# Local attention loop of a hybrid network on one core: scores of head pairs on two 64-row tiles, in a reordered step

## What is computed

```python
def local_attention(q, k, v):            # 8 heads of 64, windows of 64 tokens
    # each query sees its own window and the one before it
    sim = jnp.einsum('bhwid,bhwjd->bhwij', bq, bk)
    mask = (i < j) | (i > j + WINDOW) | (j == -1)
    sim = jnp.where(mask, -jnp.finfo(sim.dtype).max, sim)
    attn = jax.nn.softmax(sim, axis=-1)
    return jnp.einsum('bhwij,bhwjd->bhwid', attn, bv)

def _layer(x, wqkv, qs, ksc, wo, lg, lb, w1, b1, w2, b2):
    h = shift_token(x)
    q, k, v = jnp.split(h @ wqkv, 3, axis=-1)      # then to heads
    q, k = rotary_xpos(l2norm(q) * qs, l2norm(k) * ksc)
    x = x + local_attention(q, k, v) @ wo
    h = layernorm(shift_token(x)) * lg + lb
    a, g = jnp.split(h @ w1 + b1, 2, axis=-1)      # 341 wide each
    return x + (a * gelu(g)) @ w2 + b2
```

## Time and profile before

| | us |
|---|---|
| median of 3 timed runs | 2193.34 |
| lowest and highest of them | 2189.93, 2195.23 |
| the profiled execution, its device time | 2203.51 |
| the profiled execution, its span from first to last instruction | 2201.7 |

### The profile page before, as it was taken

One profiled execution on the slowest core, in us unless ns is written; L12 is line 12 of the kernel. 1 busy time (PEld: TensorE's weight loads), 2 busy tenths in 40 slices (PEclk: granted clock), 3 DMA queues, 4 the chain that ended last, 5 costly groups with the idle time before them and its releaser, 6 DMA issues.

```text
span 2201.7 us, 34222 instructions
## 1 busy us (share of the span) xinstructions
PE 1819.8 (83%) x10946; PEld 1445.6 (66%) x11003; DVE 1407.5 (64%) x3623; ACT 942.4 (43%) x2559; POOL 454.2 (21%) x350
## 2 busy tenths in 40 slices
PE   7999966654566888898888799999968988888887
PEld 6888854222355777676676677777847766776676
DVE  4655689556896666676757445655547767566673
ACT  3444422110213555546454363353225464555544
POOL 2200010000013333332424100000014324233340
PEclk9999977555778999999999899999879999999998
DMA  3000000000100000000000000000000000000000
GB/s 133 0 0 0 1 0 0 1 0 0 48 0 1 3 1 2 3 2 4 1 2 1 3 1 0 0 0 0 0 1 4 2 2 1 4 2 3 2 1 22
DMA packets 15104, 13.89 MB, mean 6 GB/s; under 512 B 11286, under 2 KB 14138, under 8 KB 14650
## 3 DMA queue, kind: packets, MB, share of 16 engines
q1 hardware_dynamic: 15034, 13.01, 1.8%
HBM read 9.87 MB, written 1.05 MB: 5 GB/s over the span
## 4 chain that ended last, share of the span: by engine, by line
PE 45%; issue 30%; DVE 16%; ACT 7%; POOL 1%; DVEq 1%; POOLq 0%; ACTq 0%
PE bank L1558 5%; PE bank L1526 4%; PE bank L1546 4%; PE bank L1695 3%; PE bank L1642 3%; PE bank L1537 3%; DVE arena_attn L916 3%; PE bank L1655 2%; PE bank L1677 2%; DVE arena_ffn L901 2%; PE bank L1720 2%; PE bank L1699 2%; DVE probT L686 2%; ACT L1264 2%; PE bank L1743 2%
## 5 line engine op out<-in xcount | busy, mean ns | idle before, releaser
L534 POOL TENSOR_TENSOR arena_ffn<-arena_ffn 128x1024 f32<-128x1024 f32 x60 | 141.5, 2359 | 561.7 <-DVE arena_ffn L901 561.7
L686 DVE COPY probT<-bank 128x512 f32<-128x512 f32 x288 | 197.1, 684 | 70.7 <-PE bank L1537 70.4
L518 POOL TENSOR_TENSOR rstd<-var,mhalf 128x2 f32<-128x2 f32 x48 | 33.4, 696 | 902.6 <-DVE var L641 902.6
L1546 PE MATMUL bank<-vF,probT 128*128 128x64 f32 x1536 | 203.0, 276 | 1.7
L1546 PEld LDWEIGHTS bank<-vF,probT 128*128 128x128 f32 x1536 | 191.3, 196 | 12.9 <-DVE probT L686 12.2
L530 POOL TENSOR_TENSOR inv<-ssq,mhalf 128x16 f32<-128x16 f32 x64 | 188.2, 2940 | 33.6 <-DVE ssq L910 29.9
L1526 PE MATMUL bank<-arena_setup 128*128 128x192 f32 (+1 forms) x1024 | 171.6, 300 | 7.2 <-ACT arena_setup L1317 5.6
L679 DVE TENSOR_REDUCE nmaxF<-bank 128x2 f32<-128x384 f32 (+1 forms) x192 | 114.7, 597 | 88.9 <-PE bank L1526 88.9
L1368 ACT ACTIVATE arena_conv<-bank,nmaxF 128x192 f32<-128x192 f32 x256 | 105.6, 420 | 147.9 <-DVE nmaxF L679 95.1
L1526 PEld LDWEIGHTS bank<-arena_setup 128*128 128x128 f32 x1024 | 154.3, 191 | 11.8 <-issue 0.4
L897 DVE TENSOR_TENSOR arena_ffn<-bank,rope 128x512 f32<-128x512 f32 x128 | 87.7, 685 | 115.0 <-ACT arena_attn L1308 115.0
(11 more groups left out here) (258 smaller groups left out, 4302.4 us busy)
## 6 DMA issues: line engine op xcount, KB each, us to landing
packF<-in_packF SPq DMA_DIRECT2D x1, 3250.0 KB
arena_history<-in_packG SPq DMA_DIRECT2D x1, 2560.0 KB, 9.0
HS<-XH SPq DMA_DIRECT2D x32, 63.5 KB
X<-in_x_tiled SPq DMA_DIRECT2D x1, 1024.0 KB, 4.8
out_dram<-X SPq DMA_DIRECT2D x8, 128.0 KB, 1.9
arena_setup<-in_const_masks_a SPq DMA_DIRECT2D x1, 512.0 KB, 5.4
arena_setup<-in_const_masks_f SPq DMA_DIRECT2D x1, 512.0 KB
HS<-XH SPq DMA_DIRECT2D x32, 0.2 KB
```

The source lines that it names most:

```text
L534: pool.tensor_tensor(t1[:, t], t1[:, t], t2[:, t], ALU.add).then_inc(sems["rope_sum"], 1)
L686: dve.tensor_copy(probT[:, u % 2], bank[4 + u % 2][:]).then_inc(sems["pt_copied"], 1)
L1546: ins = pe.matmul(o, probT[:, u % 2, n * P:(n + 1) * P], val, start=first, stop=(kt == keys // P - 1), skip_group_check=True)
```

## The change

1. Scores. The keys are stored once (keysF, one ACT copy for each token half), without zeros. A head's scores are a matmul over its own 64 rows, and `score_pair` makes units s and s + 1 together for s = 0, 2, 4: both masks, then the heads of the even unit (rows 0 to 63, bank 0) and of the odd unit (rows 64 to 127, bank 1) in turn, with one increment of the semaphore by two behind the last. It waits for the exp of unit s - 1, so that both banks are free. The latent attention stage keeps its own scores.
2. Order on PE. The transposes of the next x stand first in the step; the waits for the keys come behind the hidden gates. Both value projections move behind the transposes of the first half of y, ahead of the last value products.
3. Order on DVE. `gated` (L1021) goes ahead of the first rope part, `hidden_stats` behind the last.
4. Order on ACT. The copies to hT stand between the load of the gelu table and the gelus.
5. Bias. b2 is a 114th row of the last chunk of w2, against a row of ones in ff; L1674 is gone. POOL fills that row once per stage.

```diff
-                for j in range(2):
-                    rows_ = slice(64 * j, 64 * j + 64)
-                    ins = act.activation(keysZ[rows_, 0:4, j, t * P:(t + 1) * P],
-                                         bank[4 * t + 1][rows_].rearrange("p (h c) -> p h c", c=P), ACT.Copy)
-                ins.then_inc(sems["qkT_ready"], 1)
+                act.activation(keysF[:, :, t * P:(t + 1) * P], bank[4 * t + 1][:].rearrange("p (h c) -> p h c", c=P),
+                               ACT.Copy).then_inc(sems["qkT_ready"], 1)
...
+            def score_pair(v, i, s, mask, scores):
+
+                t, _, keys = attn_unit(s, 2)
+                width = keys - F_FROM[t]
+                pe.wait_ge(sems["exp_ready"], v.at("exp_ready", i, s))
+                for m in range(2):
+                    cols = len(attn_unit(s + m, 2)[1]) * width
+                    pe.matmul(bank[m][:, 0:cols], identb[:], mask[:, t, 0:cols], start=True, stop=True)
+                for n in range(len(attn_unit(s, 2)[1])):
+                    for m in range(2):
+                        q, k = scores(attn_unit(s + m, 2)[1][n], t, keys)
+                        ins = pe.matmul(bank[m][:, n * width:(n + 1) * width], q, k, start=False, stop=True, skip_group_check=True)
+                ins.then_inc(sems["s_ready"], 2)
...
                 def scores(h, t, keys):
-                    return qTF[:, h // 2, t * P:(t + 1) * P], keysZ[:, h // 2, h % 2, F_FROM[t]:keys]
+                    rows_ = slice(FHD * (h % 2), FHD * (h % 2) + FHD)
+                    return qTF[rows_, h // 2, t * P:(t + 1) * P], keysF[rows_, h // 2, F_FROM[t]:keys]
...
-                    if nxt and s in (7, 8):
-                        project_values(vn, ni, nl, s - 7)
                     if s == 8:
                         transpose_y(0)
+                        if nxt:
+                            for t in range(NT):
+                                project_values(vn, ni, nl, t)
...
-                    pe.matmul(bank[7][:, t * P:(t + 1) * P], ones1[:], f_at[f"b2_{l}"][0:1, :], start=True, stop=False)
                     for c in range(NCH):
-                        n = FROWS[c]
-                        ins = pe.matmul(bank[7][:, t * P:(t + 1) * P], ff[0:n, c, t * P:(t + 1) * P],
-                                        f_at[f"w2_{l}"][0:n, c * C:(c + 1) * C], start=False, stop=(c == NCH - 1))
+                        ins = pe.matmul(bank[7][:, t * P:(t + 1) * P], ff[0:FCH, c, t * P:(t + 1) * P],
+                                        f_at[f"w2_{l}"][0:FCH, c * C:(c + 1) * C], start=(c == 0), stop=(c == NCH - 1))
```

More of the change, by code:

```diff
@@ L372, in zeros_by @@
         def zeros_by(n):
-            return N_POOL_FILL + sum((plan[m] == "conv") + (plan[m] == "win" and plan[m - 1] != "mlp")
+            return N_POOL_FILL + sum(2 * (plan[m] == "win" and plan[m - 1] != "mlp")
                             for m in range(n + 1))
@@ L1469, in _ @@
                         win(n, l, NB - 1)
+                    prime(ACT.Gelu)
                     gelus(vals[n + 3], NB - 2, 1)
@@ L1511, in _, with attention @@
             credit(pe, "pt_ready", "pv_done", "hqT_psum", "lin_av")
-            def attention(v, i, units, groups, banks, mask, scores, values, between, probs=(prob, prob), origin=(0, 0)):
+            def score_pair(v, i, s, mask, scores):
[10 more added lines that the diff above has]
+                ins.then_inc(sems["s_ready"], 2)
+            def attention(v, i, units, groups, banks, mask, scores, values, between, probs=(prob, prob), origin=(0, 0), paired=False):
                 for s in range(units + 3):
-                    if s < units:
+                    if paired and s < units and s % 2 == 0:
+                        score_pair(v, i, s, mask, scores)
+                    if s < units and not paired:
                         t, heads, keys = attn_unit(s, groups)
```

40 lines of the change are left out of this document (20 added, 20 removed).

## The result

| | before | after |
|---|---|---|
| median of the timed runs, us | 2194.28 | 2341.46 |
| lowest and highest | 2189.93, 2195.74 | 2338.18, 2341.79 |
| span of the profiled execution, us | 2201.7 | 2340.0 |
| mean granted clock of PE over it | 0.909 | 0.86 |

The change makes the kernel slower: after / before is 1.067, 95% interval 1.065 to 1.069, +147 us. The forecast said slower, but 2280 us (2190 to 2325); the direction held and the size did not.

The account below looks back on a forecast made before the run. In the local step no engine is full; a ring of waits between PE, ACT, DVE and POOL bounds it. Steps 42, last layers 7, lone steps -4.5, clock 42: +87 us to 2290, less 10 for the median: 2280 (2190 to 2325).

Parts of the forecast that it names:

- Cost of the tile pairs: Scores in a local step: first pair 1.1 us, other two 0.9 each, saving 1.5 us of PE time (1.0 to 2.0).
- rival 3: The two tile streams of a pair run one after the other: +2.3 us a step, 2350 us; chance 0.05.
- The wait of 2.9 us: PE, done at 6.1 us, waits 2.9 us ahead of the second pair for the second exp, released at 9.0.
- Rival 2: Exps done before 7.5 us into the step, so PE's saving stays: -46 us, 2147 us; chance 0.13.
- Bias row and front: Front savings go into waits, second q and k projection still at 15.8 us; bias row's 1.1 us gains nothing in steady steps.
- lone steps: Four steps running alone behind the two loops: the bias row saves 1.1 us in each, 4.5 us in all.
- Lock of L909: DVE's small op (L910 before) held by POOL's later rope add for 1.35 us instead of 0.7; y 0.67 us late.
- last layers: In 14 steps POOL's final add delays the rope add and holds DVE's small op 0.5 us longer: 7 us.
- Tail and step: End of the local step: last value products done at 31.0 us, step 35.9 instead of 34.6 us, +1.3.
- The ring as a whole: Waits between engines in the local loops: 42 us over 32 steps plus 7 in last layers, with -4.5 outside.
- Rival 1: The waits come but PE's clock holds: +45 us, 2238 us; chance 0.22.
- The clock: PE at 1.2 GHz for a stretch in most local steps: 1.5 us in 28 of 32, 42 us; bounds 0 and 75.

Follow-up runs that it names:

- e9: e6 plus idle PE work, 12 mask matmuls ahead of the pair of units 2 and 3 and 6 ahead of the first value projection: 2215.3 us, ratio 1.010.
- e12: e7 plus idle PE work, 5 mask matmuls ahead of the first value projection: 2121.2 us, ratio 0.967.
- e3: The kernel before with only the score pairs on 64-row tiles and keys stored once: 2324.3 us, ratio 1.060.
- e6: The changed kernel with value projections and hidden statistics back in their old places: 2248.5 us, ratio 1.021.
- e8: The kernel before with the bias row alone: 2166.8 us, ratio 0.986.
- e1: The changed kernel with mask matmuls that no one reads put into three of PE's waits in each local step: 2255.8 us, ratio 1.029.
- e4: The changed kernel with the value projections back in their old places: 2268.3 us, ratio 1.034.
- e7: The kernel before with only the bias row and new front (x transposes first, hT copies ahead of gelus, gated ahead of rope): 2119.0 us, ratio 0.964.
- e11: e7 run again unchanged, on the same chip as e12: 2116.9 us, ratio 0.966.
- e10: e7 plus idle PE work, 3 mask matmuls ahead of unit 3 and 5 ahead of the first value projection: 2131.3 us, ratio 0.972.

## Why the prediction was right, and where it failed

- **Cost of the tile pairs: right.** 1.1 us for the first pair; it took 1.09 (849.08 to 850.17), and the gate chunk behind it 0.53 instead of the 0.43 of full matmuls, which is the 0.1 us taken for the way back. The others 0.9; 0.85 (857.13 to 857.98). The two tile streams do overlap, so rival 3 is out. The bounds of the saving were reckoned wrong: with 0.3 us a pair taken double or at nothing, 4.4 us less the three pairs gives 0.5 to 2.3, not 1.0 to 2.0. The Trainium skill's page "TensorEngine Tiling (Array Packing)" (Key Properties) says that a change of tiling mode drains the engine. These numbers contain such a drain, but no run shows it by itself.
- **The wait of 2.9 us: right,** 2.83. First exp at 5.1 us, measured 5.3; release at 9.0, measured 9.2; second q and k projection at 15.8, measured 15.9. Rival 2 (exps done before 7.5) is out. What the pairs cost in all, with their saving of PE time taken off, is 2.8 us a step with the new front (e9 against e12) and 2.2 with the old (e3).
- **Bias row and front: right as a sum, wrong by parts.** The front of the step came out as walked (15.8, measured 15.9), because the pairs' 2.2 us and the 2.0 us of front and bias row cancel. But "nothing is gained in the steady step" by the bias row is not borne out: from e3 to e6 the stretch between the second and the third pair gets 0.6 us shorter, while the wait in it grows by 0.6. The order of DVE differs between the two as well, and no run has the bias row alone with pairs, so its share is not measured exactly. e8 shows that in the kernel before the same edit is worth 1.0 us in every step. In the lone steps I took 1.1 us each; the two behind the last loop gave 1.4 together (the end went from 24.26 to 22.84 us).
- **Lock of L909: right.** 1.35 us predicted, 1.28 measured. In the last layers it is held for up to 1.96. The plain steps of e1 are 1.5 us longer than those of before. In the last layers the difference is about the same in the first loop (35.8 to 37.3) and 0.6 more in the second (34.7 to 36.8), some 4 us in all where I took 7.
- **Tail and step: right.** Last value products done at 31.0, in e1 at 31.2 (835.53 to 866.77); step 35.9, in e1 36.1; e4 and e6 give the parts.
- **The ring as a whole: 10 us too low.** Predicted +49 in the loops (42 + 7), and -4.5 outside. e1 against before gives +51 in the loops, but before had 29 us more at half clock; at 0.28 each that is 8, so the ring is +59. Rival 1, 2238 us, was this case; e1 measures it at 2256.
- **The clock: this step failed.** I took 1.5 us in 28 steps, 42 in all, with 75 as the upper bound. The loops show 84 us between after and e1, 76 of them beyond what before had paid already. The mechanism was right; the time at half clock in a step was not. I had read the price from steps of before that hold one stretch of 3.5 us at half clock and let every step have one such. In fact a steady step has 6.8 to 14 us of it: the clock falls at up to two places of a step, and a fall lasts longer. The price of a stretch was too high, which hid a part of this: 1.5 us for 3.5 us is 0.43 for each, where e1 gives 0.29. The 2.7 us behind the upper bound was partly a misreading. The step of 37.3 us in the earlier trace rows belongs to a last layer, where a step of before at full clock takes 35.8 us in the first loop, so its stretch cost 1.5 us and not 2.7. My bound of 75 then let every step have one stretch, though the text itself listed four waits in each.
- **Not foreseen:** the first step of the first loop ends 6.6 us later. From 700 us to there the granted clock is 0.89 after and 1.00 before. The sum had no term for it.

Together: 10 us (the ring), some 34 (the clock in the loops: 76 against 42) and 7 (the first step) make 51 of the 61 us between 2280 and 2341. The other 10 were taken off because the profiled execution of before lay 10 us over its median; that of the kernel after lies at its median.

What led the design astray is seen in e3 and e7. Pairs save some 1.5 us of PE time a step, but at this place PE's own work is not what the step waits for. Two banks that must both be free turn two waits of one exp each into one wait of two. At full clock that costs 2.2 to 2.8 us a step, more than front and bias row give back with pairs (2.0 us); without pairs these two give 2.6 and more.

## What to carry to other kernels

Before joining two units of work into one on the engine that stands in a ring of waits, work out when the later of the two buffers comes free: that wait replaces the earlier one and can cost more than the work that joining them saves. When PE gets new waits of 1 to 3 us in every step, price the clock by the number of such places in a step, not by one stretch a step, with some 0.3 us for each us at half clock from this kernel's rows, and let the range reach to a step that is slow at every one of them. Try the parts of a bundled change alone: the front and the bias row of this one make the kernel 78 us faster (e7 and e11), and the rest outweighed them.

## What the runs showed of the hardware

- A one-row matmul ahead of full ones cost far more than its columns: taking four such instructions out of sixteen made the hidden output 1.1 us shorter (2.46 before, 1.34 from 846.54 to 847.88 in e1), 0.28 us each where one of the others of 128 columns takes 0.112. The steps of e8 got 1.0 us shorter.
- Time at half clock cost 0.29 us of loop time for each us (after against e1) and 0.27 (e6 against e9). The Trainium skill's page "TensorE: Matmul & The Clock Gate" (HAM oscillation) reckons half of the time spent throttled as the penalty. By that rule the estimate for the 290 us of after would be 145 us; the traces give 84, and the measurement decides. The steps of e6 show most of the difference: with 6.6 us at half clock (841.21 to 877.86) PE is busy 30.70 us instead of 28.36, 0.35 us more for each, because it also waits in that time, and the step is 1.8 us longer, 0.28 for each.
- The same kernel's loops repeat to 0.2 us on two chips (954.9 and 954.7, with the same steps slow), while the stages between them, with unchanged code, took between 412.3 us (e11, at a granted clock of 0.94) and 433.1 (e3, at 0.90). The bias row can make up some 2 us of that spread of 21 us, by the steps that run alone; what sets the clock there stays open.
- The idle work showed the price of the clock and brought the kernels with pairs 85 and 33 us (e1 against after, e9 against e6). In the fastest kernel it gained nothing in total (e10 and e12 against e7 and e11).
